# Deformable-convolution and attention kernel: the last addition of a tile's weighted corners on TensorE instead of VectorE

## What is computed

```python
h = relu(bn(conv1x1(x, w1)))                     # 128 -> 32 channels
off = conv3x3(h, woff) + boff                    # 27 maps: y, x and mask of nine taps
y, x = off[y] + base_y, off[x] + base_x          # nine sampling points per pixel
samp = gather(y0, x0) * wy0 * wx0 + gather(y0, x0 + 1) * wy0 * wx1 \
     + gather(y0 + 1, x0) * wy1 * wx0 + gather(y0 + 1, x0 + 1) * wy1 * wx1
h = einsum('bckhw,ock->bohw', samp * sigmoid(mask), w2) + b2
x = relu(bn(conv1x1(relu(bn(h)), w3)) + x)       # 32 -> 128 channels
f, g, h = wf x + bf, wg x + bg, wh x + bh        # 16 channels each, 3136 pixels an image
out = (wv (h softmax(f^T g)^T) + bv) * gamma + x
```

## Time and profile before

| | us |
|---|---|
| time, median of 3 executions | 1624.76 |
| lowest, highest | 1620.49, 1626.18 |
| the profiled execution, its time | 1626.56 |
| its span, first to last instruction | 1624.7 |
| POOL busy | 1232.4 |
| PE busy (matmuls) | 1138.4 |
| DVE busy | 923.6 |
| ACT busy | 679.0 |

### The profile page before, as it was taken

How to read it: one execution, slowest core, us unless ns; L and a number is a source line. 1 busy time by engine, 2 the same in 40 slices (tenths; PEclk the granted TensorE clock), 3 DMA queues, 4 the chain that set the end, 5 groups by cost and what they waited for, 6 DMA issues and landing times.

```text
span 1624.7 us, 18271 instructions
## 1 busy us (share of the span) xinstructions
PE 1138.4 (70%) x5637; PEld 523.5 (32%) x5637; DVE 923.6 (57%) x1881; ACT 679.0 (42%) x1428; POOL 1232.4 (76%) x1674
## 2 busy tenths in 40 slices
PE   4627356444557777677777777777777686899998
PEld 2213122221223333333333333333333243344443
DVE  5344161553545657566565656656567474677782
ACT  2102031231225535355443554435544354466766
POOL 3888888888888888888888888888888888800000
PEclk9756758555568768687886786777777686799999
DMA  3232312211111111111111111111111111100000
GB/s 148 69 112 63 122 39 71 72 45 44 42 42 42 43 54 45 53 41 43 54 45 52 43 45 54 44 55 40 45 54 41 54 43 42 54 12 1 12 13 23
DMA packets 37033, 82.04 MB, mean 50 GB/s; under 512 B 15290, under 2 KB 16942, under 8 KB 36424
## 3 DMA queue, kind: packets, MB, share of 16 engines
q0 software_dynamic: 28224, 57.86, 13.0%
q1 hardware_dynamic: 8676, 22.92, 3.8%
q10 hardware_dynamic: 36, 0.10, 0.0%
HBM read 66.23 MB, written 14.59 MB: 50 GB/s over the span
## 4 chain that ended last, share of the span: by engine, by line
POOL 75%; issue 10%; PE 10%; DVE 3%; ACT 1%; DMA 1%; POOLq 0%; ACTq 0%; SPq 0%; DVEq 0%
POOL G L323 59%; POOL pad L330 16%; PE PV L478 3%; DVE mxp L949 1%; PE L2b L462 1%; PE L1b L448 1%; ACT H L695 1%; PE L2a L462 1%; PE L1a L448 1%; PE L1c L448 1%; PE T L462 1%; DVE par L1051 1%; PE M L507 1%; PE M L499 0%; PE L1a L358 0%
## 5 line engine op out<-in xcount | busy, mean ns | idle before, releaser
L323 POOL DMA_INDIRECT G<-table,IDX x882 | 961.0, 1090 | 186.0 <-issue 158.6
L929 DVE TENSOR_TENSOR G<-G,CW 128x640 f32<-128x640 f32 x196 | 145.9, 752 | 345.0 <-DMA G<-table,IDX 345.0
L695 ACT ACTIVATE H<-L2a 112x448 f32<-112x448 f32 x355 | 193.2, 544 | 286.5 <-PE L2a L462 258.9
L695 ACT ACTIVATE H<-L2b 112x448 f32<-112x448 f32 x364 | 198.7, 546 | 181.6 <-PE L2b L462 135.8
L330 POOL MEMSET pad<- 128x256 f32 x784 | 258.7, 330 | 0.6
L448 PE MATMUL L1b<-G,F 96*112 96x448 bf16 x280 | 125.0, 446 | 157.9 <-DVE mxp L949 155.9
L478 PE MATMUL PV<-H,HTc 112*32 112x448 f32 x1568 | 229.6, 664 | 1.6 <-ACT HTc L717 0.9
L949 DVE TENSOR_REDUCE mxp<-L1b 112x1 f32<-112x448 f32 x280 | 173.4, 619 | 53.8 <-PE L1b L448 41.7
L949 DVE TENSOR_REDUCE mxp<-L1a 112x1 f32<-112x448 f32 x252 | 156.0, 619 | 33.8 <-PE L1a L448 21.9
L949 DVE TENSOR_REDUCE mxp<-L1c 112x1 f32<-112x448 f32 x252 | 155.9, 619 | 31.0 <-PE L1c L448 21.2
L448 PE MATMUL L1c<-G,F 96*112 96x448 bf16 x252 | 112.7, 447 | 83.4 <-DVE mxp L949 80.5
(11 more groups left out here) (123 smaller groups left out, 1402.4 us busy)
## 6 DMA issues: line engine op xcount, KB each, us to landing
G<-table,IDX POOLq DMA_INDIRECT x882
table<-TS SPq DMA_DIRECT2D x24, 256.0 KB
out<-X SPq DMA_DIRECT2D x13, 448.0 KB, 2.5
X<-xt SPq DMA_DIRECT2D x3, 1568.0 KB, 10.8
offd<-OFS SPq DMA_DIRECT2D x28, 47.2 KB
OFG<-offd SPq DMA_DIRECT2D x13, 94.5 KB
X<-xt SPq DMA_DIRECT2D x1, 1120.0 KB, 7.5
table<-TS SPq DMA_DIRECT2D x4, 128.0 KB
```

Of the source, the lines that this page charges most:

```text
L323: eng.indirect_dma_start(G[:, j, k * 4 * CB:(k + 1) * 4 * CB], None, table[0:images * POS, :], bass.IndirectOffsetOnAxis(ap=IDX[:, g % IRI ...
L695: nc.scalar.activation(E[:, (i - SKEW) % ERING, :], l2((i - SKEW) % BLOCKS, tail)[0:KT, 0:CHUNK], ACT.Exp).then_inc(s_exp, 1)
L929: eng.tensor_tensor(rows, rows, weights.unsqueeze(2) .to_broadcast([128, n, CB]), ALU.mult).then_inc(s_mul, 1)
```

## The change

`tile_sum` is gone. `tile_pairs` now writes `S2` with left and right corners apart, as two blocks of 9 x 32 channels, and `S2` has two buffers by j even or odd; it takes over the sum's wait for `s_pt`, which tells that the transposes of the tile before last have read that buffer. `tile_in` waits for `s_s2` and makes, for each of the three pieces, two ordinary float32 products with the identity matrix: left columns with start, right columns with stop, into the same columns of bank `T`. The product with the identity transposes as the transposes did, and the bank adds the two.

```diff
-TILE_PAIRS, TILE_SUM = 2, 3
+TILE_PAIRS = 2
...
-        S2 = sb("S2", [128, TAPS, 2 * CB])
-        S = sb("S", [128, 2, TAPS * CB])
+        S2 = sb("S2", [128, 2, 2, TAPS * CB])
...
-                eng.wait_ge(s_sum, n + 1)
+                eng.wait_ge(s_s2, n + 1)
                 for t in range(3):
-                    mm = eng.transpose(T[0:96, t * 128:(t + 1) * 128],
-                                       S[:, j % 2, t * 96:(t + 1) * 96], ident)
+                    for x in range(2):
+                        mm = eng.matmul(T[0:96, t * 128:(t + 1) * 128],
+                                        S2[:, j % 2, x, t * 96:(t + 1) * 96], ident,
+                                        start=(x == 0), stop=(x == 1))
                 mm.then_inc(s_pt, 1)
...
             def tile_pairs(g, j):
                 n = TPG * g + j
                 eng.wait_ge(s_mul, 2 * (n + 1))
-                pair = G[:, j, :].rearrange("p (k a c) -> p k a c", k=TAPS, a=2)
-                eng.tensor_tensor(S2[:, :, :], pair[:, :, 0, :], pair[:, :, 1, :], ALU.add)\
+                after(eng, s_pt, n - 1 if j else n)
+                pair = G[:, j, :].rearrange("p (k a x c) -> p k a x c", k=TAPS, a=2, x=2)
+                eng.tensor_tensor(S2[:, j % 2, :, :].rearrange("p x (k c) -> p k x c", c=CB),
+                                  pair[:, :, 0, :, :], pair[:, :, 1, :, :], ALU.add)\
                    .then_inc(s_s2, 1)
-
-            def tile_sum(g, j):
-                n = TPG * g + j
-                eng.wait_ge(s_s2, n + 1)
-                after(eng, s_pt, n - 1 if j else n)
-                eng.tensor_tensor(S[:, j % 2, :].rearrange("p (k c) -> p k c", c=CB),
-                                  S2[:, :, 0:CB], S2[:, :, CB:2 * CB], ALU.add).then_inc(s_sum, 1)
...
-                    if g is not None and i - TILE_SUM in HALVES[h]:
-                        tile_sum(g, HALVES[h][i - TILE_SUM])
```

More of the change, by code:

```diff
@@ L180, in build @@
         gathered = [sem(f"gathered{j}") for j in range(TPG)]
-        s_mul, s_s2, s_sum = sem("s_mul"), sem("s_s2"), sem("s_sum")
+        s_mul, s_s2 = sem("s_mul"), sem("s_s2")
         s_pt, s_st, s_w2 = sem("s_pt"), sem("s_st"), sem("s_w2")
```

## The result

The changed kernel took 1617.74 us (median of 20 runs, 1604.14 to 1636.22) beside 1624.42 us (20 runs, 1615.02 to 1631.22) of the kernel before: a ratio of 0.9958, 95% interval 0.9937 to 0.9978. A later repetition (12 runs beside 29) gave 0.9965 [0.9943, 0.9986].

The account below looks back on a forecast made before the run. The prediction took POOL's gathers to bound the kernel: +5.6 us for a POOL stall, -3.2 for the removed sum and +3.0 for the tail gave +5.4 us, against the median 1624.76 a forecast of 1630.2 us, range 1622 to 1638.

Parts of the forecast that it names:

- What bounds the kernel: Whole span: start, 1377 us of POOL's gathers, 205 us tail; added PE work in the attention stage is covered.
- the term of the sum: POOL's gathers: removing DVE's sum shortens those it held back, -3.2 us, with ends 0 and -16.
- what follows comes earlier 0 +- 4: DVE instructions behind a sum in the same burst come 0.45 us earlier and may meet other gathers: 0 +- 4 us.
- The direct part: Nine gathers ending some 0.83 us after a sum's end, together 3.2 us above 0.95 each; the other 89 sums cost nothing.
- The forecast's own end of -16 us: Far end for the sum on POOL: 123 us of gather lengthening shared out by DVE's busy time, the sum about an eighth.
- The stall: First gather of group 3: 25.4 us delay against 20.0 us slack makes POOL wait for tile 14's pairs, +5.6 us (0 to +9).
- The rival of a rising clock: Early bursts: PE's clock rises, leaving 17 us of delay under the slack, no stall; 1624.6 us, chance 0.20.
- the same limit a group earlier: At tile 7, one group before the stall: the buffer limit meets only 13.0 us of delay and holds, so no wait there.
- The tail: After the last gather: added transposing work on PE for the last tiles costs +3.0 us, ends 0 and +6.
- Rival 3: Last group: PE bounds it, the added 2.0 us of all seven tiles reach the tail, 14 us; 1641 us, chance 0.08.
- Rival 2: POOL's gathers: held back much less, by 16 us, so the kernel is faster; 1617 us, chance 0.07.
- the prediction's own signs of error: PEclk above 0.5 from 112 to 145 and 212 to 245, chain leaving POOL before 1400, gathers' mean moving over 5 ns.

Follow-up runs that it names:

- Experiment 1: Kernel after the change, but T makes three transposes of the left columns only, right columns left out, no sum: 1610.49 us, ratio 0.9935, repeated 0.9945.
- experiment 2: Kernel before, sum kept, each transpose of the summed tile replaced by two float32 products with the identity: 1624.59 us, ratio 0.9991.
- experiment 6: Kernel before with the sum one step later in DVE's order, nothing removed: 1615.01 us, ratio 0.9928.
- experiment 4: Kernel after, but groups 0 to 2 and last group 13 keep sum and transposes: 1616.87 us, ratio 0.9945.
- experiment 3: Kernel after, but groups 0 to 2 keep sum and transposes, products in groups 3 to 13: 1609.42 us, ratio 0.9911.
- the placebo: Experiment 1 plus an unused one-operand DVE maximum over 288 elements in the sum's place: 1616.81 us, ratio 0.9940, repeated 0.9986.

## Why the prediction was wrong, point by point

**What bounds the kernel** was right in the main: POOL's gathers carried 18.3 us of the difference. But not all that DVE and PE do in the attention stage stayed hidden: in the profiled execution of after the chain left POOL at 1361, 42 us before its last gather ended; in the repetition it stayed there to the last one. Experiment 1, without products, had the same in its first execution (1356 us), so that it isn't the products alone. PE's 12 instructions a tile came as forecast (x1176), at 2.88 us instead of 2.89 at the lower clock and 1.55 instead of 1.47 at the upper, and the pairs kept their 751 ns.

**The step that failed is the term of the sum**, -3.2 us with "what follows comes earlier 0 +- 4". It measured some 10 us by experiment 1, twice. The direct part was right for the trace it was read from, nine holds of 3.2 us, and small for the second execution of the same kernel, fifteen of 6.5. What was mis-sized above all is what follows. The prediction wrote that most tiles start their first multiplication when their gather lands, "so multiplications and pairs keep their place against the next gathers". They don't: the same sum one step later on DVE, with nothing removed, took the pairs near a start from 75 and 72 to 61 and the time down by 11.3 us. DVE waits for the rows in 52 and 48 of 98 tiles before, and in 36 and 41 after; in the others it arrives from other work, and there 0.45 us less, or a step of delay, can change which gather start the pairs meet (which tiles carry the gain the traces don't separate). The pairs have 44 to 49 us in holds; a shift of a seventh of these (experiment 1) to a quarter (after), as was seen, is worth more than all sums. The bound that should have been set for that term is that of the neighbour's holds, not of the removed instruction's. The forecast's own end of -16 us did include it, with a chance of 0.07.

**The stall** was right in place, cause and releaser, and too large: 3.6 us in one execution, none in the other, where 5.6 was forecast with 0 to 9. In after the pairs of tile 14 end at 321.98 against 305.45, 16.5 us later and not 25.4. Most of that gap is no error in the price of the chain: its first T starts 5.8 us earlier in after (106.78 against 112.60), of which the missing sum explains 0.5, and from there to the end of these pairs it takes 22.3 us longer (215.2 against 192.9; 17.4 between the repetitions). Why the front comes earlier the traces don't say; over the traces with three transposes a tile the first T starts from 98.5 to 114.8 us. The rest fits T's and products of the front that ran at the upper clock. In the order of time of after:

```profile
322.75 1.38 POOL L322 DMA_INDIRECT G<-table,IDX  x1 [3.63 <-DVE S L938]
```

```profile
321.22 0.76 DVE L938 TENSOR_TENSOR S<-G 128x576 f32<-128x576 f32 x1
```

The slack was smaller too, 14 us and not 20, as POOL came there 6 us earlier: a gain on POOL in groups 0 to 2 is given back as wait when PE sets the pace. The rival of a rising clock (0.20) held in the repetition, as it was told: PEclk 0.76, some 17 us of delay, no stall; its time, 1624.6, is not what was measured. That the same limit a group earlier holds was wrong in experiment 2, where a wait of 6.95 us stood before tile 14's gathers. The 20.0 us of slack was one execution's too: the pairs of tile 14 end at 297.56 in the repetition of before, 7.9 us earlier than in the first.

**The tail** came out at +7.3 us in this execution for a forecast of +3.0, and at +0.8 between the repetitions (202.8 to 203.6). Two executions without products have tails of 208.6 (experiment 6) and 209.0 us (experiment 1 again), and experiment 4, which keeps the products out of the last group, is not better than experiment 3. The term has no size that these runs can show. Rival 3 (PE bounds the last group) happened in one execution, for 7 us; what stands out there are the two standstills of PE, 7.0 us together, which the rival did not have.

**The products in all** cost +2.3 +- 4.2 us (after beside experiment 1) or, from the ratios (0.9958 and 0.9965 beside 0.9935 and 0.9945), some 3.5 us. Forecast were 5.6 + 3.0 = 8.6. This is the second mis-sized term, and nearly as large as the first: 5 to 6 us.

**Put together**: 10 us for the sum less 3 for the products is a gain of 7, measured 6.7 (medians 1624.42 and 1617.74); forecast was -3.2 + 8.6, a loss of 5.4. Of the 12 us between them some 7 are the sum's and some 5 the products'. Rival 2's time, 1617, is what was measured; its reason, a share of the hold time by the sum's busy time, is not what was found. That the time agrees with this rival is luck. All of the prediction's own signs of error did appear: PEclk above 0.5 from 112 to 145 and from 212 to 245 (where it was 0.55 before too, so that this half of the sign told nothing), the chain leaving POOL before 1400 in one of two executions, and a gathers' mean that moved by 21 ns.

**What stays open** is how the 10 us divide into reads and place (some 5 and 6 by the holds, 3.7 and 4.7 by the times on one chip, 9.5 for the reads alone on another), and why one chip gave 6 us more to the placebo than the other. The count of pairs near a gather's start moves from 75 to 64 between before and after, and by up to 6 between two executions of one kernel; with one or two profiled executions of each the two can't be told apart more finely. That the one with the fewest, 61, isn't the fastest, and experiment 3 with 72 is as fast as any of them, says that this count is not all either. Open is also what makes one execution differ from the next. Waits of DVE and ACT as in the tail of after, over 1 us long, behind 355 us and with no releaser that the profile can match, add up to 0 and 46 us in the two executions of the placebo, to 36 and 8 in those of experiment 1, and to 108 and 46 in those of after; in the first two kernels the execution with more of them has the fewer pairs near a start. No run tests whether they are the reason.

## What to carry to other kernels

When an instruction is removed that sometimes holds up a neighbouring engine, price also its neighbours: what they hold is sensitive to their phase, and this term has to be bounded by their holds (here 44 to 49 us of pairs), not by its own (3.2 and 6.5). Take a second profile of the same kernel before trusting such a count. Before replacing such an instruction by work on a third engine, look whether one with a single SBUF operand can do it; even at 2.13 us in place of 1.2 it won 2.9% here, as long as it stays off the tail. And where added PE work sits in a serial chain of matmul, copy, matmul, expect its price to change by execution with the granted clock.

## What the runs showed of the hardware

- A DVE instruction of two SBUF operands holds a gather's instruction on POOL only if it is active close to the gather's start; the gather then ends 0.83 us after that instruction. In the stretch from 0.65 us before to 0.45 us behind the start 69 of 75 pairs held in before, further in none of 22. On who interferes the runs agree with the Trainium skill (SBUF — State Buffer, "Who interferes with whom"), which names VectorE's instructions with two SBUF inputs: the reductions with one, 2.13 us long, held nothing.
- A sum over four corners with a stride, 1152 elements in and 288 out, took 2.13 us, 1.85 ns an element, while the maxima over 448 neighbouring elements of the attention's logits took 0.62 us, 1.38 ns an element, and the placebo's over 288 in SBUF 0.44 us. They differ in operation and output too, so that the stride is not shown to be the reason.
- Between 112 and 145 us the granted clock was 0.50 with three transposes a tile (0.55 in one trace of eleven) and 0.55 to 0.76 with six products, different by execution. Experiment 2 also spread more than the kernel before on its chip, with a standard deviation of 9.9 us (7.8 over the eight runs counted) beside 3.4. For the change it is 5.5 beside 3.8 in the repetition, which is no more than the placebo's 5.8, a kernel without products.
- Six float32 products with the identity, 128 columns each, are twelve instructions and took 2.88 us at the lower clock; three transposes of the same size are three and took 0.88. Each of the nine more cost 0.22 us, and a product thus less than twice a transpose (0.48 and 0.29 us).
